# A Swin block on one core: tokens numbered by columns, and three steps of TensorE's order moved

## What is computed

```python
h = layernorm(x, norm1_g, norm1_b)
hw = h.reshape(B, 16, 8, 16, 8, C).transpose(0, 1, 3, 2, 4, 5).reshape(-1, 64, C)   # windows
qkv = hw @ qkv_w + qkv_b                        # q, k, v of 3 heads
attn = softmax(q * SCALE @ k^T + bias[None])    # bias = rel_bias_table[REL_IDX], 64 x 64 a head
out = (attn @ v).reshape(Bw, 64, C) @ proj_w + proj_b
x = x + windows_back(out)
h2 = layernorm(x, norm2_g, norm2_b)
return x + gelu(h2 @ fc1_w + fc1_b) @ fc2_w + fc2_b
```

## Time and profile before

| | |
|---|---|
| median of 3 runs | 1095.75 us |
| the profiled execution | 1095.25 us |
| its span, first to last instruction | 1093.5 us |
| mean granted clock of TensorE | 0.99 of full speed |
| TensorE (PE) busy | 1039.8 us, 95% |
| its weight loads (PEld) | 921.9 us, 84% |
| VectorE (DVE) busy | 803.0 us, 73% |
| GpSimd (POOL) busy | 759.6 us, 69% |
| ScalarE (ACT) busy | 693.9 us, 63% |
| DMA | 38.25 MB, mean 35 GB/s |

### The profile page before, as it was taken

One profiled execution on the slowest core, in us unless ns is written; L12 is line 12 of the kernel. 1 busy time (PEld: TensorE's weight loads), 2 busy tenths in 40 slices (PEclk: granted clock), 3 DMA queues, 4 the chain that ended last, 5 costly groups with the idle time before them and its releaser, 6 DMA issues.

```text
span 1093.5 us, 26409 instructions
## 1 busy us (share of the span) xinstructions
PE 1039.8 (95%) x7366; PEld 921.9 (84%) x7366; DVE 803.0 (73%) x2301; ACT 693.9 (63%) x1347; POOL 759.6 (69%) x1174
## 2 busy tenths in 40 slices
PE   1999999999999999999999999998899999999997
PEld 0788888888888888888888888887799999999997
DVE  4677777777777777777777777767577777777773
ACT  1566666667666676666666666664476666766664
POOL 5577666776567765677666676565578888988881
PEclk9999999999999999999999999999799999999999
DMA  1011001010011110111100111000011111111111
GB/s 43 28 34 36 33 29 42 32 37 33 29 39 34 36 35 29 36 36 35 36 29 32 40 34 36 31 15 29 1 37 39 39 43 43 43 43 43 43 39 48
DMA packets 24807, 38.25 MB, mean 35 GB/s; under 512 B 4119, under 2 KB 20698, under 8 KB 24794
## 3 DMA queue, kind: packets, MB, share of 16 engines
q1 hardware_dynamic: 24722, 37.90, 11.0%
q10 hardware_dynamic: 72, 0.20, 0.1%
HBM read 25.50 MB, written 12.58 MB: 35 GB/s over the span
## 4 chain that ended last, share of the span: by engine, by line
PE 79%; ACT 13%; issue 3%; POOL 1%; DVE 1%; DMA 1%; ACTq 1%; SPq 0%; DVEq 0%; POOLq 0%
PE scores_ps L596 16%; PE scores_ps L541 12%; PE mixed_ps L556 11%; PE probs_t_ps L548 6%; PE x_ps L526 6%; PE x_ps L589 6%; ACT tokens_t L767 5%; PE x_ps L529 5%; ACT k_blocks L776 4%; PE x_ps L583 4%; PE x_ps L562 3%; ACT probs L789 3%; PE x_ps L533 3%; PE x_ps L573 3%; PE x_ps L567 3%
## 5 line engine op out<-in xcount | busy, mean ns | idle before, releaser
L464 POOL TENSOR_TENSOR lowered<-biased,row_top 128x384 f32<-128x384 f32 x256 | 212.2, 829 | 247.5 <-DVE row_top L982 245.6
L770 ACT ACTIVATE probs_t<-probs_t_ps 128x384 f32<-128x384 f32 x256 | 126.9, 496 | 256.0 <-PE probs_t_ps L548 254.4
L377 POOL TENSOR_TENSOR rstd<-small,minus_half 128x4 f32<-128x4 f32 (+1 forms) x160 | 242.7, 1528 | 0.0
L556 PEld LDWEIGHTS mixed_ps<-v_blocks,probs_t 128*128 128x128 f32 x1536 | 195.6, 192 | 39.9 <-ACT probs_t L770 21.8
L541 PE MATMUL scores_ps<-k_blocks,q_blocks 96*128 96x192 f32 x1024 | 224.8, 343 | 1.6 <-DVE q_blocks L970 1.6
L556 PE MATMUL mixed_ps<-v_blocks,probs_t 128*128 128x66 f32 x1536 | 206.6, 271 | 4.8 <-ACT probs_t L770 1.7
L978 DVE TENSOR_TENSOR biased<-scores_ps,pos 128x384 f32<-128x384 f32 x256 | 142.7, 557 | 81.4 <-PE scores_ps L541 77.1
L596 PEld LDWEIGHTS scores_ps<-wfc,hidden 128*128 128x128 f32 x1536 | 181.6, 192 | 5.9 <-issue 0.3
L596 PE MATMUL scores_ps<-wfc,hidden 128*128 128x96 f32 x1536 | 180.4, 274 | 0.0
L541 PEld LDWEIGHTS scores_ps<-k_blocks,q_blocks 96*128 96x128 f32 x1024 | 163.2, 193 | 3.7 <-DVE q_blocks L970 2.1
L982 DVE TENSOR_REDUCE row_top<-biased 128x6 f32<-128x384 f32 x256 | 141.6, 553 | 8.9
(11 more groups left out here) (100 smaller groups left out, 1576.6 us busy)
## 6 DMA issues: line engine op xcount, KB each, us to landing
x<-in_x SPq DMA_DIRECT2D x128, 96.0 KB
out<-x SPq DMA_DIRECT2D x128, 96.0 KB
x_in<-in_x SPq DMA_DIRECT2D x244, 48.0 KB
x_second<-in_x SPq DMA_DIRECT2D x8, 48.0 KB
x_in<-in_x ACTq DMA_DIRECT2D x4, 48.0 KB
pos_in<-in_L_conv_rel_bias_table SPq DMA_DIRECT2D x8, 10.6 KB
wproj<-in_L_conv_proj_w SPq DMA_DIRECT2D x6, 3.0 KB
wfc_in<-in_L_conv_fc_w SPq DMA_DIRECT2D x2, 36.0 KB
```

The source lines that it names most:

```text
L377: pool.tensor_tensor(rstd[:, groups], small[:, 7, groups], minus_half[:, groups], ALU.pow).then_inc(step, 1)
L464: pool.tensor_tensor(lowered[:, k % 2, :, :], biased[:, k % 2, :, :], broadcast(row_top[:, k % 2, :], 2, TOK), ALU.subtract).then_inc(lowe ...
L556: mm = pe.matmul(mixed_ps[:, at:at + MIX], probs_t[:, h, :], v_blocks[:, part, u, h, :], start=True, stop=True)
L770: act.activation(probs_t[:, :, :], probs_t_ps[:, 0:HEADS * 128].rearrange("p (h q) -> p h q", h=HEADS), ACT.Copy).then_inc(probs_t_ok, 1)
```

## The change

Tokens in a window get the number 8 j + i, column first, where it was 8 i + j. `tokens_out` and `heads_out` write and read by it, the table's loads take one column pj each, and `pos_all` is copied with its last two axes exchanged. On TensorE, slot 3 does `turn_tokens` ahead of `turn_heads`; `project_k(x_ps[2], 0)` moves from slot 5 to slot 6 and gets a wait on `heads_t_ok`; `project_heads(x_ps[0], 1)` moves from slot 6 to slot 7, ahead of what stands there. The helper `token_view` is gone. No other engine's order changes.

```diff
@@ block.sync
-            for pi in range(WIN):
-                load(pos_in[WIN * pi:WIN * pi + WIN, :, :], bass.AP(
-                    table.tensor, REL * pi, [[1, WIN], [TABLE, HEADS], [1, REL * (WIN - 1) + WIN]]), table_in)
+            for pj in range(WIN):
+                load(pos_in[WIN * pj:WIN * pj + WIN, :, :], bass.AP(
+                    table.tensor, pj, [[REL, WIN], [TABLE, HEADS], [1, REL * (WIN - 1) + WIN]]), table_in)
@@ block.tensor, fill
                 if k == 3:
-                    if not first:
-                        wait(pe, k_ok, 2 * n + 2)
-                        wait(pe, heads_ok, 4 * n)
-                        turn_heads(x_ps[2], 1)
                     if not last:
                         wait(pe, q_ok, 2 * n + 2)
                         wait(pe, normed_ok, 2 * n + 3)
...
                         turn_tokens(1)
+                    if not first:
+                        wait(pe, k_ok, 2 * n + 2)
+                        wait(pe, heads_ok, 4 * n)
+                        turn_heads(x_ps[2], 1)
@@
                         project_q(x_ps[1], 0)
-                        wait(pe, k_ok, 2 * n + 2)
-                        project_k(x_ps[2], 0)
-                if k == 6 and not first:
-                    project_heads(x_ps[0], 1)
+                if k == 6 and not last:
+                    wait(pe, k_ok, 2 * n + 2)
+                    wait(pe, heads_t_ok, 2 * n)
+                    project_k(x_ps[2], 0)
                 if k == 7:
+                    if not first:
+                        project_heads(x_ps[0], 1)
@@ block.scalar
             def tokens_out(half):
-                source = x_ps[half][0:C2, :].rearrange("c (j t) -> c j t", j=HALF)
-                act.activation(token_view(tokens_t[0:C2, :, :], half), source, ACT.Copy).then_inc(tokens_ok, 1)
+                source = x_ps[half][0:C2, :].rearrange("c (j ka i) -> c ka j i", j=HALF, i=WIN)
+                view = tokens_t[0:C2, :, :].rearrange("c k (a j i) -> c (k a) j i", a=2, j=WIN)
+                act.activation(view[:, :, HALF * half:HALF * half + HALF, :], source, ACT.Copy).then_inc(tokens_ok, 1)
@@
             def heads_out(bank, part):
                 at = 2 * WIN * UNITS * part
-                act.activation(heads_t[0:C2, :, at:at + 2 * WIN * UNITS],
-                               bank[0:C2, :].rearrange("c (ubi j) -> c j ubi", j=WIN), ACT.Copy).then_inc(heads_t_ok, 1)
+                act.activation(heads_t[0:C2, :, at:at + 2 * WIN * UNITS].rearrange("c j (ua i) -> c j ua i", i=WIN),
+                               bank[0:C2, :].rearrange("c (ua j i) -> c j ua i", j=WIN, i=WIN), ACT.Copy
+                               ).then_inc(heads_t_ok, 1)
@@ block.vector
             wide = bass.AP(pos_in, 0, [[HEADS * (REL * (WIN - 1) + WIN), TOK], [REL * (WIN - 1) + WIN, HEADS],
-                                       [REL, WIN], [1, WIN]])
+                                       [1, WIN], [REL, WIN]])
```

More of the change, by code:

```diff
@@ L254, in broadcast @@
             return ap.unsqueeze(axis).to_broadcast(shape)
-        def token_view(tokens, half):
-            view = tokens.rearrange("c k (ai j) -> c j (k ai)", j=WIN)
-            return view[:, HALF * half:HALF * half + HALF, :]
         block = ctx.enter_context(nc.Block())
@@ L706, in _ @@
             pe.matmul(probs_t_ps[:, 0:HEADS * TOK], flip[:, :, :].rearrange("p b q -> p (b q)"),
-                      pos_all[:, :, :, :].rearrange("p h i j -> p (h i j)"), start=True, stop=True).then_inc(pos_mm, 1)
+                      pos_all[:, :, :, :].rearrange("p h j i -> p (h j i)"), start=True, stop=True).then_inc(pos_mm, 1)
             batches(pe, body)
```

## The result

The changed kernel takes 1068.19 us (median of 4 runs, 1065.27 to 1070.11) against 1095.48 before (median of 4, 1094.02 to 1095.81). The ratio is 0.9751 with a 95% interval of 0.9727 to 0.9776: 2.5% faster. The forecast was 1068.8.

What follows compares the result with a forecast made beforehand. TensorE sets the pace, losing 0.87 us a batch in waits. 29 x (0.59 + 0.28 + 0.05) = 26.7, with the setup 27.2, less the end 26.9, gives 1068.8 us; 8-in-10 range 1065.0 to 1078.0.

Steps and rivals of the forecast that it cites:

- Slot 5 by the numbering, 0.59 a batch: TensorE's slot 5: the faster tokens' write ends the wait before the queries' projection, winning 0.59 us in 29 batches.
- The tokens' write at 0.59 us: ScalarE's `tokens_out` falls from 1119 ns to 0.59 us a call; bounds 0.58 and 1.12.
- Slot 3, 0.28 a batch: TensorE's slot 3: turning tokens first removes the wait for `k_out(1)` ahead of the heads, winning 0.28 us in 29 batches.
- 0.05 a batch from the mix of slot 6: Slot 6's mix to scores shortens from 0.67 to 0.62 us once `project_heads` no longer stands ahead of it.
- Margins: Slack left in the new order, the smallest 0.36 us for `heads_t` ahead of `project_heads` in slot 4.
- The load of `x_in`: Its trigger comes about 1.6 us earlier, gaining some 0.7 us of slack; VectorE's waits in slot 3 mostly go.
- Ends: Setup 0.5 us shorter, batches 0 and 1 zero, last batch 0.3 us longer with bounds -0.9 and +1.5.
- Rival C: Slot 3's heads, mix and scores wait behind late `normed` from GpSimd: 9 us slower, 1104 us; chance 0.03.

Runs made afterwards that it cites:

- cols_only: Changed kernel with TensorE's order put back as before the change, so the column numbering alone: 1077.05 us, ratio 0.9857 to the kernel before.
- order_only: Kernel before with TensorE's three moves alone, rows numbered as before: 1086.48 us, ratio 0.9921.
- slot3_only: Kernel before with only slot 3's order changed, tokens turned ahead of heads: 1085.35 us, ratio 0.9902.
- cols_slot3: Changed kernel without the moves between slots 5, 6 and 7: 1067.15 us, ratio 0.9745 to the kernel before; five runs again, 1067.69 us.
- norm_late: Changed kernel with GpSimd's scaling of the next batch's tokens one slot later, in slot 2: 1114.69 us, one run.
- last_batch: Numbering and slot 3's order, without the other moves, plus VectorE statistics one slot later and GpSimd's root in halves in the last batch: 1066.06 us.

## Why the prediction was right, point by point

- **Slot 5 by the numbering, 0.59 a batch.** Right in size and cause: 22.93 to 22.34 in cols_only, no gain there from the new order in order_only.
- **The tokens' write at 0.59 us.** Right: 585 ns for runs of 8 read and 32 written. `heads_out` stayed at 588. The copy into `pos_all`, which now reads floats 60 bytes apart, takes 464 ns where it took 345; the matmul that reads it starts some 8 us after it, so nothing waited.
- **Slot 3, 0.28 a batch.** Right in its cause, and 0.04 too small: 0.32 in slot3_only (22.61). I measured the wait and left out the restart behind it, which I had counted in slot 5.
- **0.05 a batch from the mix of slot 6.** Wrong. The distance from slot 6's mix to the scores is still 0.68 (492.56 to 493.24), so it was not `project_heads` ahead of it that made the 0.67. Its weights come late in both kernels. In this slot the load begins 0.12 us after ScalarE's copy of the probabilities ends (491.90 + 0.49 = 492.39), in slot 5 0.05 after (489.39 + 0.49 = 489.88, then 489.93), and the program has one more wait in even slots, for `heads_ok`. I take that as the reason; no run tested it:

```profile
489.93 0.76 PEld L551 LDWEIGHTS mixed_ps<-v_blocks,probs_t 128*128 128x128 f32 x6 [0.58 <-ACT probs_t L768]
...
492.51 0.74 PEld L551 LDWEIGHTS mixed_ps<-v_blocks,probs_t 128*128 128x128 f32 x6 [0.65 <-DVE heads L991]
```

- In slot 7 the mix now comes 0.89 after the values' start, where it was 0.86 in the kernel before (489.40 to 490.26). So the moves cost 0.04 in an ordinary batch where I had a gain of 0.05, and 0.2 us over all 29, since they also end the late `heads` of slot 4. Of 0.92 a batch 0.873 came, 1.4 us less in all. That the moves are worth next to nothing held, the sign didn't.
- **Margins.** `project_heads` in slot 4 has 0.18 us, not 0.36. I took the wanted time of the matmul, but its weights are loaded ahead of it, 0.10 here (486.52, matmuls at 486.62), and from ScalarE's end to a weight load that waits for it there were 0.05 in the row above. The new stop then cost 0.36 a batch, for the 0.2 of my expectation.
- **The load of `x_in`.** The lead grew as forecast: VectorE had waited in 27 batches, and in the changed kernel it waits for that load in none after batch 1. The two traces without the moves still have 27 and 26 such waits, so it is the moves that end them.
- **Ends.** What is shown of the setup is that the wait for its tokens went from 1.3 to 0.8 us. That batch 2 began 0.59 earlier, for a forecast of 0.5, is luck: in other traces of the changed schedule it is 1.12 and 0.43 earlier, and in order_only, without the numbering, 0.94 (77.25). The last batch with the MLP phase gave 1.5 where I had put a loss of 0.3. That is outside my bound of -0.9 on this side, and also within what one kernel's executions differ by (348.07 and 350.40 in cols_slot3 twice). The clock doesn't explain it, its mean over the first 45 us of that stretch is 0.77 in both traces; the cause is open. So two errors of 1.4 and 1.8 us cancelled, and that the total came within 1 us of the forecast owes to that. The gain itself, 25.3 of 27.4 us, is the two stops.
- **Rival C.** Its price was right, 1.31 a batch measured in norm_late for 1.33 expected, and it did not occur: both halves of `normed` are ready at 482.30 and wanted at 483.66, 1.36 us early.

## What to carry to other kernels

Measure a stop from start to start and against a batch that doesn't have it, and count its restart; then give each stop its own edit and test them one by one. Here two edits of the four made 2.5%, and spreading work over slots made nothing, since the stop stood ahead of what was moved. In a copy of fp32 from PSUM to SBUF on ScalarE, write at least two neighbouring floats together and put the stride on the read, which was free at every stride measured here (8, 32 and 256 bytes).

## What had not been expected of the hardware

The changed kernel's first four runs spread over 4.8 us against 1.8 before (in five later ones over 1.8), and its traces differ only ahead of batch 2 and behind batch 30. TensorE's granted clock falls in the last batch of every version: its mean over the 45 us from there is 0.77 to 0.81 in every trace. In the changed kernel:

```profile
730.00:735.00 5.00, 5.00 (x23) 4.87 (x22) 2.91 (x15) 2.76 (x6) 5.00 (x4) 0.50 0.00 0
```

That is 1.2 GHz, the lower level. In the kernel before it is there too (0.50 from 765 to 770 us), after TensorE stood still for 3.48 us; in the changed one it is there already at the mix of slot 2 of the last batch, which takes 1.32 us after a stop of 1.35:

```profile
726.12 1.32 PE L551 MATMUL mixed_ps<-v_blocks,probs_t 128*128 128x66 f32 x6 [1.35 <-issue]
```

In the second trace of the same kernel the mix behind the same stop of 1.35 takes 0.85, at full clock, and so it does in the kernel before. What tips it stays open. The early fall cost nothing that can be seen, since from batch 31 to the end the first trace takes 348.86 us and the second 349.69. A low clock ahead of batch 2 goes with more: in last_batch and norm_late it is 0.65 and 0.66 from 50 to 60 us, and batch 2 begins 5 to 7 us later. It isn't all that varies there, for in cols_only, with 0.83 from 30 to 40 us, batch 2 begins at 75.41, the second earliest of all traces.

A difference below 0.3% between versions of this kernel is best read from the whole stretch of batches 2 to 30 in the trace: 639.64, 639.64 and 639.65 us for the changed schedule, 639.46 and 639.42 without the moves. A single batch misleads, since they are not all alike.
